# A Mamba scan whose input is built transposed: columns of B scale du^T, TensorE turns it into PSUM, and the product with C moves from VectorE to GpSimd

## What is computed

```python
x = in_proj_w @ hidden_states;  u = silu(causal_conv4(x) + conv_b)      # (512 channels, 512 steps)
x_dbl = x_proj_w @ u            # rows: dt_lo (16), Bm (16), Cm (16)
delta = softplus(dt_proj_w @ dt_lo + dt_proj_b)
for t in range(512):            # state: 512 channels x 16
    state = state * exp(delta_t * A) + (delta_t * u_t) * B_t
    y_t   = sum_n state[:, n] * C_t[n]
y = (y + D * u) * silu(z);  x = x + y^T
x = x + moe_ffn(layernorm(x))   # top 2 of 8 experts
```

## Time and profile before

| | us |
|---|---|
| median of 3 runs | 1381.13 (1376.32 to 1383.25) |
| span of the profiled execution | 1381.1 |
| DVE busy in that span | 868.8 (63%) |
| PE busy | 1116.1 (81%) |
| POOL busy | 606.3 (44%) |
| ACT busy | 520.5 (38%) |
| first scan of `mamba_block` starts | 56.96 |
| last product with C ends | 617.3 |
| `ffn_block` begins its DMAs | 645.04 |

### The profile page before, as it was taken

The page is one execution under the profiler, slowest core; times in us unless marked ns, Lnnn a source line. Parts: engine busy times, 40 slices in busy tenths (PEclk is TensorE's granted clock), DMA queues, the critical chain, the costliest instruction groups (busy, mean ns, idle before and its releaser), DMA issues.

```text
span 1381.1 us, 18552 instructions
## 1 busy us (share of the span) xinstructions
PE 1116.1 (81%) x4156; PEld 745.3 (54%) x4156; DVE 868.8 (63%) x745; ACT 520.5 (38%) x697; POOL 606.3 (44%) x424
## 2 busy tenths in 40 slices
PE   4657667677668756763499999999999999999994
PEld 2223222223223322323478888888888888888883
DVE  3799999999999999993732434343253434324321
ACT  3754456555654565222221323232231323213210
POOL 0398498668976798630201222222122222223211
PEclk8688888899778888895599999999999999999998
DMA  5333342336234524334521424242142433414210
GB/s 158 139 122 121 124 137 91 123 121 230 72 110 139 197 91 148 113 104 166 193 107 46 167 101 167 106 164 98 38 160 99 143 124 104 166 48 167 92 40 30
DMA packets 68892, 168.01 MB, mean 122 GB/s; under 512 B 9039, under 2 KB 11599, under 8 KB 68865
## 3 DMA queue, kind: packets, MB, share of 16 engines
q1 hardware_dynamic: 59824, 139.41, 29.4%
q0 software_dynamic: 9040, 28.32, 6.3%
HBM read 343.60 MB, written 18.35 MB: 262 GB/s over the span
## 4 chain that ended last, share of the span: by engine, by line
PE 49%; DVE 2%; DMA 1%; issue 0%; POOL 0%; ACT 0%; POOLq 0%; DVEq 0%
PE hp L1433 10%; PE hp L1432 10%; PE hp L1434 10%; PE yp L1432 5%; PE yp L1434 5%; PE yp L1433 5%; PE tp L1473 2%; PE xp L1426 1%; PE hp L1417 1%; PE yp L1481 0%; DMA work<-xln_dram,index 0%; DMA work<-out_dram,acc_index 0%; DMA out_dram<-work,out_index 0%; DVE R L1299 0%; POOL index L1045 0%
## 5 line engine op out<-in xcount | busy, mean ns | idle before, releaser
L293 POOL TENSOR_TENSOR ring<-du,bc 128x1024 f32<-128x1024 f32 x128 | 361.6, 2848 | 149.2 <-DMA bc<-bcs 80.9
L681 PE MATMUL yacc<-ring,ident 128*128 128x512 f32 x512 | 292.8, 711 | 139.0 <-DVE ring L544 138.2
L532 DVE TENSOR_TENSOR_SCAN ring<-dA,ring 128x1024 f32<-128x1024 f32 x128 | 290.9, 2275 | 6.8 <-ACT dA L356 3.5
L681 PEld LDWEIGHTS yacc<-ring,ident 128*128 128x128 f32 x512 | 106.4, 224 | 308.4 <-DVE ring L544 209.1
L356 ACT ACTIVATE dA<-delta,Acol 128x511 f32<-128x511 f32 (+1 forms) x256 | 165.7, 681 | 223.5 <-DVE ring L532 223.3
L1432 PE MATMUL hp<-w_hi,xT_hi 128*128 128x512 f32 x592 | 237.5, 401 | 0.9 <-DVE xT_lo L1329 0.9
L1433 PE MATMUL hp<-w_lo,xT_hi 128*128 128x512 f32 x592 | 236.6, 400 | 0.0
L1434 PE MATMUL hp<-w_hi,xT_lo 128*128 128x512 f32 x592 | 232.9, 393 | 0.0
L544 DVE TENSOR_TENSOR ring<-ring,bc 128x1024 f32<-128x1024 f32 x128 | 217.9, 1707 | 0.0
L1350 DVE TENSOR_TENSOR work<-hp,work 128x512 f32<-128x512 f32 x74 | 51.0, 690 | 232.3 <-PE hp L1434 194.4
L1069 POOL COPY out_index<-out_tab 128x1 uint32 x37 | 6.7, 181 | 356.4 <-DVE work L1336 356.4
(11 more groups left out here) (177 smaller groups left out, 1186.5 us busy)
## 6 DMA issues: line engine op xcount, KB each, us to landing
stage<-in_L_ffn_w_kernel_dram SPq DMA_DIRECT2D x160, 1024.0 KB
stage<-in_L_ffn_wo_kernel_dram SPq DMA_DIRECT2D x78, 1024.0 KB
bc<-bcs SPq DMA_DIRECT2D x128, 512.0 KB, 4.5
xall<-in_x_dram SPq DMA_DIRECT2D x1, 4096.0 KB, 15.1
xln_dram<-xlnb SPq DMA_DIRECT2D x4, 1024.0 KB, 7.8
out_dram<-xall SPq DMA_DIRECT2D x4, 1024.0 KB, 9.4
ctx_rows<-in_ctx_dram SPq DMA_DIRECT2D x4, 512.0 KB, 4.9
work<-xln_dram,index POOLq DMA_INDIRECT x39, 3.8
```

The costliest lines, as they stand in the source:

```text
L293: g_.tensor_tensor(ring[:, n % RING, :].rearrange("p (e l) -> p e l", e=2), cols(du, b, h * 2 * L, 2 * L).rearrange("p (e l) -> p e l", e= ...
L532: v_.tensor_tensor_scan(ring[:, n % RING, :], dA[n % 2][:, :, :].rearrange("p e l -> p (e l)"), ring[:, n % RING, :], 0.0, ALU.mult, ALU.a ...
L681: last = t_.matmul(yacc[:, e, :], ident[:, :], ring[:, n % RING, e * L:(e + 1) * L], start=False, stop=(n == UPH - 1))
```

## The change

The state-space stage is written anew. What differs, unit by unit:

- **Input of the scan.** `du` is transposed once for each half (`du_T`: PE into `pp`, ACT copies to `duT`), and so are the rows of x_proj's output (`x_dbl_T`, to `xdT`). In the transposed form a row of B is a column, one scalar for each partition. A unit's input is then four pieces of 128x256, duT times that scalar (`piece`): two on ACT (as an activation with a scale), one on POOL, one on DVE, into one of 4 slots of `dBT`. PE turns it with eight 128x128 transpositions into one of two PSUM tiles `dB` (`turn_in`).
- **dA** goes to one of 3 tiles in SBUF instead of two in PSUM.
- **DVE** scans dA (SBUF) and dB (PSUM) into a ring of 6; the product with C is now POOL's (`times_c`). B is not sent through DRAM any more, so the broadcast DMAs carry only C (half the bytes).
- **Softplus.** The bias of dt comes in as a 17th row of the dt projection; POOL's subtraction and ACT's Relu become one DVE instruction from PSUM (`relu`, 2 for each half). `du`, `delta` and `spw` keep fewer copies.
- **Layer norm.** The start value of the reciprocal root is a bit trick on DVE and three Newton steps on POOL (14 small instructions) instead of Ln and Exp on ACT; the statistics of x (`stats_1`, 16 + 16 instructions of DVE) move from ahead of the first scan to unit 4.
- **Order.** All four batches are written out; the steps for other batches stand at new unit numbers.

The core of the diff. A piece of a unit's input, and ScalarE's list (UPB is 32 units a batch, DAS 3, BTS 4):

```diff
+        def piece(eng, engine, q, t, done, act=False):
+
+            b, h, n = UNIT[q]
+            if n == 0:
+                eng.wait_ge(duT_ok, 2 * b + h + 1)
+                eng.wait_ge(xdT_ok, b + 1)
+            if q >= BTS:
+                eng.wait_ge(dB_full, q - BTS + 1)
+            o, i, s = dBT[:, q % BTS, t, :], duT[:, h, t, :], xdT[:, b % 2, t, 2 * DS + n:2 * DS + n + 1]
...
+            def exp_dA(q):
+                b, h, n = UNIT[q]
+                if n == 0:
+                    act.wait_ge(delta_ready, 2 * b + h + 1)
+                if q >= DAS:
+                    act.wait_ge(scan_done, q - DAS + 1)
...
+                for s in range(UPB):
+                    q = b * UPB + s
+                    if q + 2 < NU:
+                        pieces(q + 2)
+                    exp_dA(q)
+                    if s == 0:
+                        dt_abs(b, 1)
+                        soft(b, 1)
+                    if s == 2 and nxt:
+                        ctx_T(b + 1)
+                    if s == 3:
+                        soft_log(b, 1)
+                    if s == 7 and nxt:
+                        tap(b + 1, 0)
+                        tap(b + 1, 1)
+                    if s == 8:
+                        du_T(b, 1)
+                    if s == 10 and nxt:
+                        tap(b + 1, 2)
+                        tap(b + 1, 3)
...
+                    if s == 12 and nxt:
+                        silu_u(b + 1)
+                        silu_z(b)
+                    if s == 13 and nxt:
+                        x_dbl(b + 1)
+                    if s == 14 and nxt:
+                        x_dbl_T(b + 1)
+                    if s == 16 and nxt:
+                        dt_abs(b + 1, 0)
+                        soft(b + 1, 0)
+                    if s == 18 and rest:
+                        xln(b - 1)
+                    if s == 19 and nxt:
+                        soft_log(b + 1, 0)
+                    if s == 23 and rest:
+                        gate_T(b - 1, 0)
+                        gate_T(b - 1, 1)
...
+                    if s == 25 and nxt:
+                        du_T(b + 1, 0)
```

```diff
+            def scan(q):
+                dve.wait_ge(exp_done, q + 1)
+                dve.wait_ge(dB_full, q + 1)
+                if q >= RING:
+                    dve.wait_ge(acc_done, q - RING + 1)
```

GpSimd's list has at each unit times_c(q), then its piece of unit q+4; the softplus' add and product with u follow at units 4 and 5 and at 20 and 22, the Newton steps at 8 or 11. TensorE's list (LAG is 3) has y_T at units 4 and 20, gate_T at 22 and 23, and:

```diff
+            def turn_in(q):
+
+                for done in (bt_act, bt_pool, bt_dve):
+                    pe.wait_ge(done, q + 1)
+                if q >= 2:
+                    pe.wait_ge(scan_done, q - 1)
...
+                    if q + 2 < NU:
+                        turn_in(q + 2)
+                    if q >= LAG:
+                        acc(q - LAG)
+                    if s == 0:
+                        dt_proj(b, 1)
+                    if s == 2 and nxt:
+                        ctx_T(b + 1)
...
+                    if s == 6 and nxt:
+                        in_proj(b + 1, (0, 1))
+                    if s == 7:
+                        du_T(b, 1)
+                    if s == 9 and nxt:
+                        in_proj(b + 1, (2, 3))
+                    if s == 12 and nxt:
+                        x_proj(b + 1)
+                    if s == 13 and nxt:
+                        x_dbl_T(b + 1)
+                    if s == 15 and nxt:
+                        dt_proj(b + 1, 0)
...
+                    if s == 24 and rest:
+                        logits_of(b - 1)
+                    if s == 25 and nxt:
+                        du_T(b + 1, 0)
```

More of the change, by code:

```diff
@@ L334, in _ @@
+            rstd_2(NB - 1)
         @block.scalar
@@ L511, in _ @@
-            turn(0, TURN0, 0, rest=False)
-            with act.Fori(1, NB - 1) as b:
-                turn(b, LOOP, b - 1)
-            turn(NB - 1, LAST, 0, nxt=False)
-            guess_2(NB - 1)
+                tap(0, eb)
+            silu_u(0)
+            x_dbl(0)
+            x_dbl_T(0)
+            dt_abs(0, 0)
+            soft(0, 0)
+            soft_log(0, 0)
+            du_T(0, 0)
+            act.wait_ge(consts_ok, 1)
+            act.wait_ge(zeros_ok, 1)
+            pieces(0)
+            pieces(1)
@@ L647, in _ @@
-            turn(0, TURN0, 0, rest=False)
-            with dve.Fori(1, NB - 1) as b:
-                turn(b, LOOP, b - 1)
-            turn(NB - 1, LAST, 0, nxt=False)
+                last.then_inc(dve_step, 1)
+                dve.wait_ge(dve_step, 4 + 4 * b + 2)
+                guess(rs2, mv2, 4 + 4 * b + 2, guess2)
+            for i in range(DAS):
+                last = v_.memset(dA[:, i, :, 0:1], 0.0)
+            last.then_inc(zeros_ok, 1)
+            conv(0, (0, 1))
+            conv(0, (2, 3))
@@ new lines, in _ @@
+            for b in range(NB):
+                nxt, rest = b + 1 < NB, b > 0
+                for s in range(UPB):
+                    q = b * UPB + s
+                    scan(q)
+                    if q + BTS - 1 < NU:
+                        piece(dve, v_, q + BTS - 1, 3, bt_dve)
+                    if s == 2:
+                        loss(b, 1)
+                        relu(b, 1)
+                    if s == 3 and rest:
+                        drain_y(b - 1, 1)
+                    if s == 4 and not rest:
+                        stats_1()
+                    if s == 6 and rest:
+                        add_y(b - 1, 1)
+                    if s == 7 and nxt:
+                        conv(b + 1, (0, 1))
+                    if s == 8 and rest:
+                        stats_2(b - 1)
+                    if s == 10 and nxt:
+                        conv(b + 1, (2, 3))
+                    if s == 17 and nxt:
+                        loss(b + 1, 0)
+                        relu(b + 1, 0)
+                    if s == 19:
+                        drain_y(b, 0)
+                    if s == 22:
+                        add_y(b, 0)
+                    if s == 25 and rest:
+                        logit_copy(b - 1)
```

899 lines of the change are left out of this document (440 added, 459 removed).

## The result

The changed kernel takes 1456.9 us (median of 4 runs, 1453.7 to 1457.4) against 1380.2: 1.055 times as long [1.052, 1.057]. The prediction said 1441, within 1370 to 1500, and slower. The profiled execution spans 1455.6 us, 74.5 more than the one of before.

A forecast was written before the change was run, and what follows sets the result against it. VectorE's list bounded the kernel; afterwards round trips would. The profiled 1381 us plus 38 (four batches, 598 against 560), 4 (first scan), 1 (end) and 17 (TensorE's clock) gave 1441 us, range 1370 to 1500.

The forecast's parts named there:

- trips: Between scans: turn_in, accumulation, task, copies, two pieces, exp in a chain; VectorE's waits sum to 58.9 us a middle batch.
- the trip of unit 26: Wait before scan 26: logits 4.5, turn_in and accumulation, transpositions of du, copies, pieces, exp; 10.8 us.
- Taps and convolution: Units 7 and 10: they wait for the projection one unit ahead; 4.9 and 3.6 us.
- the Ln at unit 20: ScalarE's Ln again, behind four layer-norm instructions (2.9); VectorE waits 1.5 us.
- VectorE's 103 us of own work: Middle batch: scans and pieces 80, the rest convolution, statistics, gatings, loss, relu, adds of y and gaps; down from 139.
- rival 2: VectorE's pieces queue behind GpSimd's products, 8 us a batch: 1471 us; chance 0.25, same sign, within the forecast range.
- The 1459 that stood beside it: Time if the skill's port-exclusion rule holds, with VectorE's piece nearer 0.2 than 0.3: 1441 + 30 - 12.
- its higher level: TensorE's clock at 2.4 GHz, against 1.2 at the lower level; its work in a middle batch then 111 us.
- 17 for the clock: TensorE's links in the round trips, 142 us, cost 27 more at granted clock 0.84, 10 already counted: +17 us.
- 1, engine sums: Round trips hide and TensorE's 111 us rules, 118 a batch with friction: 1298 us, faster; chance 0.14.
- 3, the lower level throughout: Gaps keep TensorE at 1.2 GHz for most of the stage: 1556 us, half of the time 1485; chance 0.08.
- 4: The step does not do what it says: VectorE scans slower from PSUM; not counted, no chance given.

The follow-up runs named there:

- the kernel with two pieces: The changed kernel with GpSimd's piece of every unit moved to VectorE, which then makes two; 1598.5 us.

## Why the prediction came out as it did

**Right.** What bounds the kernel after: trips, put down to ScalarE's dA. Waits of the second batch against the forecast, in us:

| unit | said | measured |
|---|---|---|
| 1 | 9.4 | 8.64 |
| 3 | 7.2 | 6.38 |
| 4 | 2.0 | 2.15 |
| 7 and 10 | 8.5 | 5.6 |
| 13 | 5.1 | 5.28 |
| 14, 15 | 3.1 | 3.1 |
| 17 | 6.7 | 7.02 |
| 20 | 1.5 | 0 |
| 24, 25 | 4.6 | 4.6 |
| 26 | 10.8 | 6.3 |
| drain of y, a turn_in | 0 | 2.8 |
| batch (length less busy) | 58.9 | 52.4 |

The experiment with the exps two ahead returned 73.6 of the 76.7 us, so the cause is shown and not only its rows. The term of the waits that was too dear by most is the trip of unit 26: 4.5 was counted for the logits, and they have 2.65 in it. Of these 2.17 are the wait of their copy, at unit 25, so half of the 4.6 measured there is not the copies of gate_T for which 4.6 was said: that row agrees by luck. Taps and convolution were too dear by 3 and the Ln at unit 20 by all of its 1.5. The two longest waits were to be at units 1 and 26: in the third batch they are (9.07 and 8.01), in the second unit 17 comes before unit 26.

**The step that failed: VectorE's and GpSimd's pieces.** VectorE's 103 us of own work was 113. Its piece was taken at 0.30; alone it is busy for 0.33 and takes 0.25 from start to start, but all 128 (three ahead of the first scan) took 85.9 us, 44 above 128 x 0.33: 11 a batch. The text had this as rival 2, at 8 a batch, and did not take it as the likeliest, because a convolution instruction with an operand in PSUM shows no wait; the pieces have no operand there. GpSimd's piece was given 0.45 within bounds of 0.3 and 0.8, a quarter of the product; it costs 0.95. Four times fewer columns are 2.5 times cheaper, not 4. The two together take a free unit to 3.26 once VectorE has caught up with GpSimd, and it is 2.44 before that, where 2.6 to 3.0 had been said. The Trainium skill's rule (VectorE: DVE Perf Modes, the perf-mode tier table; SBUF — State Buffer, Who interferes with whom), by which rival 2 is the truth, agrees with the trace: 0.33 alone, 1.1 or 2.4 inside a product. The 1459 that stood beside it is 2 us from the time, and that is luck: with the 44 us that the queueing cost instead of 30, and 0.25 for the piece, it would be 1441 + 44 - 6 = 1479, and the waits that were too dear bring it back down.

**The other engines.** A middle batch has 126 to 128 us of TensorE, where 111 was said for its higher level. The two links in every unit are as priced there: 0.88 and 1.72 from start to start in TensorE's rows above, where 0.87 and 1.72 were taken. After a wait the same eight transpositions are busy for 1.94 instead of 1.06; how much of the difference to 111 is that was not separated. GpSimd has 119 where 103 was said, 16 of it by its piece; ScalarE's 99 is the 100 that was said.

**The sum.** Said: 157, 162, 162, 117, and 17 for the clock, 615. Measured 170.0, 165.5, 166.3, 124.1, 625.9, clock included. A middle batch is 10 of own work above and 6.5 of waits below the forecast, clock included: two errors of opposite sign, so that 1441 lies as near as 16 us to 1457 is in part luck. Batch 0, at a granted clock of 0.80, is 13 above, the last 7. First scan +6.5 (said +4), end +2.5 (said +1). What the lower level of the clock costs by itself was not separated by any run, so the 17 us for it are not shown. The 140.1 for a batch of the kernel before is a mean: its middle batches were 142.6 and 142.8, its last 134.3. The sum goes by all four and is not touched by that.

**Rivals.** 1, engine sums: it needed exps far enough ahead, and by its working would then give 1298. The kernel that has them gave 1383, so even there TensorE's sum isn't the rule; the waits for taps, softplus, y and logits stay, and VectorE's pieces. 3, the lower level throughout: the granted clock was 0.80 to 0.94. 4: the scan takes 2.28 with its second operand in PSUM, beside GpSimd or not.

## What to carry to other kernels

Before work is moved off a saturated engine, count for each engine how many units lie between a step and its reader: a hidden trip costs nothing while the engine ahead is full, and shows as soon as work leaves it (the first trip of the second batch: 8.64 us, 5.40 with one more unit between, nothing with two). Issuing the step that all wait for two units earlier, with two more buffers, was worth 74 us here. The price of an operation that another engine can hold up is not its time alone but the length of what can be in front of it, and who starts first decides: the same piece cost 0.33 ahead of the product and 2.4 behind it. A wait that is removed from one reader is a gain only where the next one in line isn't as late: 127 us of waits went for 74 us of time.

## What the runs showed of the hardware that was not expected

- A GpSimd multiplication of 128x256 by a column of scalars takes 0.95 us beside 2.36 for a product of two tensors of 128x1024.
- VectorE's same instruction takes 0.33 us alone; started inside a GpSimd product it ends 0.15 us behind it (123 of 123 in the kernel with two pieces), and nothing counts that as idle.
- Released by the same scan, VectorE's next instruction starts 0.15 us ahead of GpSimd's: one piece gets in free, and the second took 2.4 to 2.5 us in 121 of 128 units.
- The scan with its second input in PSUM takes 2.25 to 2.29 us in the eight profiles looked at, whatever GpSimd does.
